# Softmax products moved from VectorE to GpSimd in every pair of a decoder layer, with GpSimd's own order changed around them

## The chip, the cores and the metric

One core of one Trainium2 chip. The metric is the device time of one execution in microseconds (us). In this document PE is TensorE's matrix multiply and PEld its weight load, DVE is VectorE, ACT is ScalarE, POOL is GpSimd, and SP is the engine that only issues DMAs.

## What is computed

One decoder layer on 16 sequences of 56 tokens with width 512, each with its own context of 1500 rows:

```
x = x + self_attention(layernorm(x))          # 32 heads of 16, 8 key/value heads, causal, softmax
x = x + cross_attention(layernorm(x), ctx)    # 16 heads, latent of 32, softmax over 1500 rows
x = x + ffn(layernorm(x))                     # one 512x512 product, a LoRA per sequence, bias
```

The part of the softmax that matters here is that of the self attention: row maximum, subtraction, exponential, row sum, reciprocal of the sum, and the product of the exponentials with it. The layer norm is (x - m) / sqrt(v + 1e-5) over 512 values.

## The kernel before, in words

The 16 sequences go in eight pairs, two sequences on 128 partitions (PAIRS is 8, B is 16). The whole is one software pipeline written out by hand: `run_bodies` calls `body(i)` for i from 0 to 8 on each engine, and a body has twelve steps g (0 to 11). In body i the cross attention of sequences 2i-1 (g 0 to 5) and 2i (g 6 to 11) runs, and between its pieces the list `STEPS` places the small operations of the self attention of pair n = i+1 and the end (output, ffn) of pair i-1. Every engine walks the same lists in the same order, so an engine that waits holds all that stands behind in its own order. Semaphores order the engines among each other.

The cross attention of a sequence is 24 units, numbered b * 24 + g * 4 + t, 12 for each half of the heads. For each unit PE makes scores (L741, into one of two PSUM banks `st_ps`), ACT takes the exponential (L993) into one of 8 slots of `p_ring`, PE multiplies by the context (L756) four units at a time, and POOL adds the slot onto `acc`, from which the denominators are made later (L1281). `add_up(b, half, since, until)` (L1264) is POOL's list of adds for a half: 11 adds, k from 1 to 11, where k = 1 takes two slots. ACT may write a slot again, 8 units later, only when its add is done (L992). PE also makes the pieces of the row maxima of the coming cross attention (L784, three banks `mx_ps`), 21 for each sequence, and DVE reduces each (L1210).

The self attention of pair n = i+1 in body i: PE makes the scores in steps SA and SB (g 3, L586), DVE adds the mask (L1123); then in two halves, k = 0 and 1, DVE takes the maximum (L1169) and subtracts it (L1171), ACT takes the exponential (SE0 and SE1 in g 4, L912), DVE sums (L1179), takes the reciprocal (L1184) and multiplies (L1186): `softmax_end`, called for SN0 at the end of g 4 and SN1 in g 5. PE transposes the product in g 6, steps P0 and P1 from the first half and P2 and P3 from the second (L594 to L604, recorded as L510). Two tables say which halves POOL does instead: `POOL_SHIFTS` for the subtraction (`shift`, L1299) and `POOL_SCALES` (L151) for the product (`scale`, L1306). In `POOL_SCALES` stand (0, 0) and (1, 0) alone, both done before the pipeline runs full. Where (n, k) is in it, DVE leaves the product out, POOL waits for DVE's reciprocal (`soft_n`, L1308), and PE waits for POOL (`scaled_po`, L595) in front of P0 or P2.

The three layer norms of each pair need 1/sqrt: POOL makes it in `power(which, n)` (L1284), three operations on one column each (L1289, L1292, L1296); the first waits for DVE's statistics (`mv`, L1072). ACT then normalises (L875, steps N0, N1, N2) and PE transposes the result. For the first norm (which = 0) that is step T1 in g 1 of the body. For the second (which = 1, the norm in front of the cross attention) the statistics come after step W1 in g 8 (L1132, L1068 to L1074), N1 stands in g 9 of ACT's list, and PE's T2 with the products CQ and H behind it in g 9 as well (L621 to L641).

POOL's order in a full body before the change is: `power(0, i+1)`, the 22 adds of sequence 2i-1, the 11 adds of the first half of 2i, `power(1, i+1)`, three adds, `power(2, i-1)`, the other eight adds.

Of the kernel before, what the change touches and what calls it, by code (L numbers as in the profile page):

```python
# [33 lines left out]
PAIRS = B // 2  # L34
# [113 lines left out]


POOL_SHIFTS = [(0, 0), (1, 0), (1, 1)]  # L150
POOL_SCALES = [(0, 0), (1, 0)]  # L151


LAST_STEPS = {6: ["XC"], 7: ["DN", "Y"], 8: ["DT"], 9: ["YT"], 10: ["T3"], 11: ["F1", "Fh", "F2"]}
# [9 lines left out]
def pool_adds(b, half):  # L164

    return ADDS * (b * 2 + half - sum(h < (b, half) for h in DVE_HALVES + [PE_HALF]))
# [14 lines left out]
def decoder_layer(nc, x, ctx_t, wq, wk, wv, wo, wq_d, w_qk, wkv_d, wv_u, gate_t, kern, bias,  # L181
                  lora_a, lora_b, lora_as, lora_bs, out):
    with ExitStack() as stack:
# [321 lines left out]
        def _(pe):  # L505
# [32 lines left out]
            def step(name, n, i=0, g=0):  # L538
# [50 lines left out]
                elif name in ("P0", "P1", "P2", "P3"):  # L589
                    r = int(name[1])  # L590
                    if r == 0:

                        pe.wait_ge(ct_sb, 2 * n + 1)
                    if r % 2 == 0 and (n, r // 2) in POOL_SCALES:  # L594
                        pe.wait_ge(scaled_po, POOL_SCALES.index((n, r // 2)) + 1)  # L595
                    elif r % 2 == 0:
# [465 lines left out]
        def _(ve):  # L1062
# [111 lines left out]
            def softmax_end(n, k):  # L1174
# [5 lines left out]
                ve.wait_ge(soft_n, 6 * n + 3 * k + 1)  # L1180
                if (n, k) in POOL_SCALES:
                    ve.reciprocal(inverse, total).then_inc(soft_n, 2)
# [79 lines left out]
        def _(po):  # L1262

            def add_up(b, half, since=1, until=ADDS):  # L1264

                if (b, half) in DVE_HALVES:
                    return
                if 0 <= b < B:
                    base = pool_adds(b, half)
                    dst = acc[:, b // 2 % 2, half * 8:(half + 1) * 8, b % 2 * SLOT:b % 2 * SLOT + S]  # L1270
                for k in range(since, until + 1):
                    if 0 <= b < B:
                        unit = (b * 2 + half) * 12 + k
                        po.wait_ge(exp_done, unit + 1)
                        if k == 1:

                            first = p_ring[:, (unit - 1) % PR, :].rearrange("p (h s) -> p h s", s=S)
                        else:
                            po.wait_ge(acc_done, base + k - 1)
                            first = dst  # L1280
                        po.tensor_tensor(dst, first, p_ring[:, unit % PR, :].rearrange("p (h s) -> p h s", s=S),  # L1281
                                         ALU.add).then_inc(acc_done, 1)

            def power(which, n):  # L1284

                if not 0 <= n < PAIRS:
                    return
                po.wait_ge(ln[which], (3 * n + 2, 4 * n + 3, 5 * n + 4)[which])
                po.tensor_tensor(rstd[:, which, 0:1], mv[:, which, 1:2], eps_col[:, :], ALU.add)\  # L1289
                    .then_inc(ln_eps[which], 1)  # L1290
                po.wait_ge(ln_eps[which], n + 1)
                po.tensor_tensor(rstd[:, which, 1:2], rstd[:, which, 0:1], minus_half[:, :], ALU.pow)\  # L1292
                    .then_inc(ln_pow[which], 1)
                po.wait_ge(ln_pow[which], n + 1)
                po.wait_ge(ln_neg[which], n + 1)
                po.tensor_tensor(rstd[:, which, 2:3], mv[:, which, 2:3], rstd[:, which, 1:2], ALU.mult)\  # L1296
                    .then_inc(ln_shift[which], 1)

            def shift(n, k):  # L1299

                po.wait_ge(soft, 4 * n + 2 * k + 2)
                rows = p1[:, k * 2 * G:(k + 1) * 2 * G, 0:S]
                po.tensor_tensor(rows, rows, sm[:, 0, k * 2 * G:(k + 1) * 2 * G].unsqueeze(2)
                                 .to_broadcast([128, 2 * G, S]), ALU.subtract).then_inc(shifted_po, 1)

            def scale(n, k):  # L1306

                po.wait_ge(soft_n, 6 * n + 3 * k + 3)  # L1308
                rows = p1[:, k * 2 * G:(k + 1) * 2 * G, 0:S]
                po.tensor_tensor(rows, rows, sm[:, 2, k * 2 * G:(k + 1) * 2 * G].unsqueeze(2)  # L1310
                                 .to_broadcast([128, 2 * G, S]), ALU.mult).then_inc(scaled_po, 1)
# [3 lines left out]
            def make(instruction):  # L1315

                made[0] += 1
                instruction.then_inc(pool_c, 1)
                po.wait_ge(pool_c, made[0])
# [31 lines left out]
            power(1, 0)  # L1351

            def body(i):
                power(0, i + 1)
                if i == 0:

                    po.wait_ge(eff_out, 32)
                    make(po.memset(acc[:, :, :, :], 1.0))
                    assert made[0] == ALL_MADE
                    for half in range(2):  # L1360
                        shift(1, half)
                    scale(1, 0)

                if i < PAIRS:
                    for half in range(2):
                        add_up(2 * i - 1, half)
                add_up(2 * i, 0)
                power(1, i + 1)
                add_up(2 * i, 1, until=3)
                power(2, i - 1)  # L1370
                add_up(2 * i, 1, since=4)

            run_bodies(body)


# [38 lines left out]
```

## Time and profile before

| what | value |
|---|---|
| median of 3 runs | 643.24 us |
| lowest, highest | 636.33, 643.40 us |
| the profiled execution, its own time | 636.64 us |
| span in its trace, first to last instruction | 634.8 us |
| mean granted TensorE clock | 0.984 |
| busy in the span: PE, DVE, ACT, POOL | 576.5, 404.4, 323.2, 426.6 us |

The times of rows in the trace count from the start of the span. The three runs lie at two levels, one at 636.33 us and two near 643.3 us; the profiled execution is near the lower one. A full body takes about 71.5 us (the power of the second norm comes at 236.26 us in body 2 and at 522.48 us in body 6). In timeline rows the columns are start, duration (both us), engine, line, operation, output and inputs, shapes, count; in brackets the idle time of the engine before and what ended it.

### The profile page before, as it was taken

To read this page: it belongs to the slowest core of one execution; us is meant where nothing else is said; L and a number is where in the kernel's file an instruction comes from. 1 tells how busy PE (TensorE), PEld (TensorE's weight loads), DVE (VectorE), ACT (ScalarE), POOL (GpSimd) and SP (SyncE) were. 2 spreads that over 40 slices of the span, in tenths; PEclk is the share of its full clock that TensorE was granted. 3 is DMA by queue.
4 is the path that set the end of the run, shared out by engine and by line. 5 is a ranking of instruction groups with operands and counts; after the bars stand their busy time and mean duration, and the time that the engine had idled before them with its cause. 6 is when DMAs were issued, how large, how long until landed. Compare 5 with 4: busy or idle time off the path is not lost.

```text
span 634.8 us, 11587 instructions
## 1 busy us (share of the span) xinstructions
PE 576.5 (91%) x4164; PEld 310.1 (49%) x4164; DVE 404.4 (64%) x696; ACT 323.2 (51%) x680; POOL 426.6 (67%) x414
## 2 busy tenths in 40 slices
PE   8887797999999899999999999999999899986886
PEld 7435343545446445545446444545446445433444
DVE  2536772688746955688746955688746965757532
ACT  1421445457544745557544745557544745564561
POOL 6202477589748888589748888588748878798000
PEclk9997898999999999999999999999999999999899
DMA  8959602651067201751059101751059101200000
GB/s 322 413 119 351 228 16 52 240 199 42 8 205 263 65 8 34 273 199 44 7 165 325 42 10 34 272 199 43 5 168 329 42 7 34 59 14 0 24 3 14
DMA packets 31579, 77.40 MB, mean 122 GB/s; under 512 B 11297, under 2 KB 24961, under 8 KB 29218
## 3 DMA queue, kind: packets, MB, share of 16 engines
q1 hardware_dynamic: 30854, 75.27, 35.0%
q10 hardware_dynamic: 668, 1.40, 0.6%
q8 instruction: 33, 0.54, 0.4%
q14 instruction: 24, 0.20, 0.1%
HBM read 58.92 MB, written 2.88 MB: 97 GB/s over the span
## 4 chain that ended last, share of the span: by engine, by line
PE 54%; DVE 23%; ACT 5%; SPq 5%; POOL 4%; issue 4%; DMA 4%; ACTq 1%; POOLq 0%; DVEq 0%
PE st_ps L741 9%; PE mx_ps L784 9%; PE pv_ps L756 8%; DVE mx_p L1210 7%; PE mi_ps L510 4%; PE mi_ps L522 4%; POOL acc L1281 4%; ACT p_ring L993 3%; DVE p L1123 2%; DMA x3n<-in_lora_b 2%; PE mi_ps L614 2%; DVE stats L1068 2%; SPq L422 2%; DVE p L1171 2%; PE mi_ps L618 2%
## 5 line engine op out<-in xcount | busy, mean ns | idle before, releaser
L1281 POOL TENSOR_TENSOR acc<-acc,p_ring 125x448 f32<-125x448 f32 x290 | 349.8, 1206 | 49.0 <-ACT p_ring L993 9.8
L1210 DVE TENSOR_REDUCE mx_p<-mx_ps 128x1 f32<-128x500 f32 x336 | 210.8, 671 | 109.2 <-PE mx_ps L784 108.1
L993 ACT ACTIVATE p_ring<-st_ps 125x448 f32<-125x448 f32 x372 | 184.3, 543 | 139.6 <-PE st_ps L741 132.9
L741 PE MATMUL st_ps<-q_st,c_st 98*125 98x448 f32 x372 | 144.7, 428 | 10.2 <-ACT p_ring L993 9.2
L784 PE MATMUL mx_ps<-c_st,q_st 96*128 96x500 f32 x336 | 139.6, 446 | 11.7 <-DVE p L1123 4.4
L741 PEld LDWEIGHTS st_ps<-q_st,c_st 98*125 98x125 f32 x372 | 64.6, 188 | 98.4 <-ACT p_ring L993 76.2
L756 PE MATMUL pv_ps<-p_ring,c_nat 125*32 125x448 f32 x768 | 93.5, 559 | 1.9 <-ACT ox L871 1.0
L784 PEld LDWEIGHTS mx_ps<-c_st,q_st 96*128 96x128 f32 x336 | 62.1, 192 | 44.3 <-DVE mx_p L1210 19.0
L1289 POOL TENSOR_TENSOR rstd<-mv,eps_col 128x1 f32<-128x1 f32 x24 | 5.0, 207 | 115.7 <-DVE mv L1072 115.2
L529 PE MATMUL mi_ps<-ctx_sb,wkv_sb 128*32 128x375 f32 x480 | 46.0, 504 | 3.8 <-DVE p L1123 3.8
L1159 DVE TENSOR_TENSOR x3n<-mi_ps,x 128x512 f32<-128x512 f32 x8 | 5.5, 691 | 53.9 <-PE mi_ps L725 53.9
L1281 POOL TENSOR_TENSOR acc<-p_ring 125x448 f32<-125x448 f32 x29 | 34.0, 1174 | 1.6 <-ACT p_ring L993 1.6
L871 ACT ACTIVATE qt<-mi_ps 128x512 f32<-128x512 f32 x16 | 9.6, 597 | 46.4 <-PE mi_ps L522 41.6
L522 PEld LDWEIGHTS mi_ps<-xnt,wq_sb 128*128 128x128 f32 x256 | 30.8, 192 | 0.8
L522 PE MATMUL mi_ps<-xnt,wq_sb 128*128 128x112 f32 (+1 forms) x256 | 30.8, 274 | 0.0
L756 PEld LDWEIGHTS pv_ps<-p_ring,c_nat 125*32 125x32 f32 x768 | 15.4, 108 | 30.0 <-issue 22.1
L1186 DVE TENSOR_TENSOR p<-p,sm 128x896 f32<-128x896 f32 x14 | 26.0, 1858 | 0.5
L529 PEld LDWEIGHTS mi_ps<-ctx_sb,wkv_sb 128*32 128x32 f32 x480 | 13.0, 112 | 25.0 <-issue 17.8
L1123 DVE TENSOR_TENSOR p<-mi_ps,cmask 128x448 f32<-128x448 f32 x32 | 18.4, 617 | 6.5 <-PE mi_ps L586 6.5
L871 ACT ACTIVATE ct_f<-mi_ps 128x375 f32<-128x375 f32 x15 | 7.2, 483 | 26.4 <-PE mi_ps L529 20.8
L871 ACT ACTIVATE p1t<-mi_ps 128x512 f32<-128x512 f32 x32 | 17.6, 604 | 4.1 <-PE mi_ps L510 4.1
L510 PE MATMUL mi_ps<-ident,p 128*128 128x128 f32 x128 | 18.0, 275 | 1.3 <-ACT p1t L871 0.3
(146 smaller groups left out, 678.7 us busy)
## 6 DMA issues: line engine op xcount, KB each, us to landing
ctx_sb<-in_ctx_t SPq DMA_DIRECT2D x16, 3000.0 KB, 11.2
c_st<-ct_hl SPq DMA_DIRECT2D x192, 46.9 KB, 2.3
q_st<-q_hl SPq DMA_DIRECT2D x90, 56.0 KB, 2.0
x_sb<-in_x SPq DMA_DIRECT2D x8, 256.0 KB, 2.8
out_y<-x3n SPq DMA_DIRECT2D x16, 112.0 KB
wq_sb<-in_wq SPq DMA_DIRECT2D x2, 512.0 KB, 6.0
kern_sb<-in_lora_a SPq DMA_DIRECT2D x1, 1024.0 KB, 14.5
wo_sb<-in_wo SPq DMA_DIRECT2D x1, 1024.0 KB, 17.4
```

What stands on the lines that cost most here:

```text
L510: last = pe.transpose(bank_[:, c * 128:(c + 1) * 128], src[:, c * 128:(c + 1) * 128], ident[:, :])
L522: last = mm(rows_of(o[:, r * 128:(r + 1) * 128], n), wq_sb[:, c, r * 128:(r + 1) * 128], rows_of(xnt[:, c, :], n), start=(c == 0), stop=(c ...
L529: last = mm(o[t * L:(t + 1) * L, 0:KT], wkv_sb[:, c, :], ctx_sb[:, slot, c, t * KT:(t + 1) * KT], start=(c == 0), stop=(c == CH - 1))
L741: mm(st_bank(unit)[0:KC, 0:HALF], c_st[:, b % 4, t * KT + k * KC:t * KT + (k + 1) * KC], q_st[:, b // 2 % 2, b % 2, half * HALF:(half + 1) ...
L756: last = mm(pv_ps[t * L:(t + 1) * L, 0:HALF], c_nat[:, b % 4, k, t * L:(t + 1) * L], p_ring[:, unit % PR, :], start=(k == 0), stop=(k == K ...
L784: mm(mx_ps[(b * PIECES + p) % MXB][:, 0:KP], q_st[0:96, b // 2 % 2, b % 2, j * 128:(j + 1) * 128], c_st[0:96, b % 4, k * KP:(k + 1) * KP], ...
L871: return act.activation(dst, src, ACT.Copy, scale=scale)
L993: act.activation(p_ring[:, unit % PR, :], st_bank(unit)[0:KC, 0:HALF], ACT.Exp, scale=float(L) ** -0.5).then_inc(exp_done, 1)
L1123: ve.tensor_tensor(rows[:, j:j + 2, half, :, 0:S], mi_ps[half][:, 0:G * S].rearrange("p (r g k) -> p r g k", r=2, g=G // 2), mask, ALU.add ...
L1186: ve.tensor_tensor(rows, rows, inverse.unsqueeze(2).to_broadcast([128, 2 * G, S]), ALU.mult)\
L1210: ve.tensor_reduce(mx_p[:, p:p + 1], mx_ps[unit % MXB][:, 0:KP], AX.X, ALU.max).then_inc(red_done, 1)
L1281: po.tensor_tensor(dst, first, p_ring[:, unit % PR, :].rearrange("p (h s) -> p h s", s=S), ALU.add).then_inc(acc_done, 1)
```

## The change

The table `POOL_SCALES` is longer, so that the 13 halves (1, 1), (2, 0), (2, 1) to (7, 1) have their products on POOL; DVE keeps that of (0, 1) alone. POOL's body is reordered: in bodies 1 to 7 the first add of sequence 2i-1 stands ahead of `power(0, i+1)`; in bodies 1 to 6 `scale(i+1, 0)` stands between the adds k = 5 and 6 of the second half of 2i-1, and `scale(i+1, 1)` between k = 7 and 8. In body 0 `scale(1, 1)` stands behind `scale(1, 0)`.

```diff
-POOL_SCALES = [(0, 0), (1, 0)]
+POOL_SCALES = [(0, 0)] + [(n, k) for n in range(1, PAIRS) for k in range(2)]
...
             def body(i):
-                power(0, i + 1)
                 if i == 0:
+                    power(0, 1)
 
                     po.wait_ge(eff_out, 32)
                     make(po.memset(acc[:, :, :, :], 1.0))
                     assert made[0] == ALL_MADE
                     for half in range(2):
                         shift(1, half)
-                    scale(1, 0)
-
-                if i < PAIRS:
                     for half in range(2):
-                        add_up(2 * i - 1, half)
+                        scale(1, half)
+
+                if 0 < i < PAIRS:
+                    add_up(2 * i - 1, 0, until=1)
+                    power(0, i + 1)
+                    add_up(2 * i - 1, 0, since=2)
+                    add_up(2 * i - 1, 1, until=5)
+                    if i + 1 < PAIRS:
+                        scale(i + 1, 0)
+                    add_up(2 * i - 1, 1, since=6, until=7)
+                    if i + 1 < PAIRS:
+                        scale(i + 1, 1)
+                    add_up(2 * i - 1, 1, since=8)
                 add_up(2 * i, 0)
                 power(1, i + 1)
                 add_up(2 * i, 1, until=3)
```

## Rows read from the trace of the kernel before

**Rows 1.** The page: busy time of each engine, and the chain that ended last.

```profile
PE 576.5 (91%) x4164; PEld 310.1 (49%) x4164; DVE 404.4 (64%) x696; ACT 323.2 (51%) x680; POOL 426.6 (67%) x414
...
PE 54%; DVE 23%; ACT 5%; SPq 5%; POOL 4%; issue 4%; DMA 4%; ACTq 1%; POOLq 0%; DVEq 0%
```

**Rows 2.** The waits of the whole span: who waited, total, times, longest.

```profile
POOL rstd L1289 <- DVE mv L1072: 115.2, 17, 35.5
...
PEld mx_ps L784 <- DVE mx_p L1210: 19.0, 42, 2.8
...
ACT p_ring L993 <- POOL acc L1281: 6.2, 7, 2.5
```

**Rows 3.** One line's instructions: duration min/median/max in ns, first and last start.

```profile
L1281 POOL TENSOR_TENSOR acc<-acc,p_ring x290: 1127/1141/1988, 79.4 to 583.8; 125x448 f32<-125x448 f32 x145
...
L1186 DVE TENSOR_TENSOR p<-p,sm x14: 1449/1868/2128, 23.0 to 503.9; 128x896 f32<-128x896 f32 x14
...
L1310 POOL TENSOR_TENSOR p<-p,sm x2: 1690/1690/1691, 22.5 to 75.7; 128x896 f32<-128x896 f32 x2
```

**Rows 4.** Timeline of POOL in body 2 (k = 5 first), 208.6 to 239 us.

```profile
208.57 1.15 POOL L1281 TENSOR_TENSOR acc<-acc,p_ring 125x448 f32<-125x448 f32 x1
...
209.86 3.93 POOL L1281 TENSOR_TENSOR acc<-acc,p_ring 125x448 f32<-125x448 f32 x2
...
214.28 6.33 POOL L1281 TENSOR_TENSOR acc<-acc,p_ring 125x448 f32<-125x448 f32 x4 [0.49 <-ACT p_ring L993]
...
220.57 1.16 POOL L1281 TENSOR_TENSOR acc<-p_ring 125x448 f32<-125x448 f32 x1
221.87 12.70 POOL L1281 TENSOR_TENSOR acc<-acc,p_ring 125x448 f32<-125x448 f32 x10
236.26 0.19 POOL L1289 TENSOR_TENSOR rstd<-mv,eps_col 128x1 f32<-128x1 f32 x1 [1.69 <-DVE mv L1072]
```

**Rows 5.** Timeline of DVE in body 2: the end of the softmax.

```profile
213.17 1.07 DVE L1179 TENSOR_REDUCE sm<-p 128x16 f32<-128x896 f32 x1
214.27 0.25 DVE L1184 RECIPROCAL sm<-sm 128x16 f32<-128x16 f32 x1
214.56 1.81 DVE L1186 TENSOR_TENSOR p<-p,sm 128x896 f32<-128x896 f32 x1
216.30 1.07 DVE L1179 TENSOR_REDUCE sm<-p 128x16 f32<-128x896 f32 x1
...
217.69 1.92 DVE L1186 TENSOR_TENSOR p<-p,sm 128x896 f32<-128x896 f32 x1
```

**Rows 6.** Timelines of PE and ACT in body 2: P2 and P3, a piece, T2, and N1.

```profile
219.93 1.06 PE L510 MATMUL mi_ps<-ident,p 128*128 128x128 f32 x8
...
237.59 0.47 PE L784 MATMUL mx_ps<-c_st,q_st 96*128 96x500 f32 x1
238.25 0.66 PE L510 MATMUL mi_ps<-ident,xn 128*128 128x128 f32 x4 [0.20 <-ACT xn L875]
...
237.38 0.82 ACT L875 ACTIVATE xn<-x_sb,rstd 128x512 f32<-128x512 f32 x1
```

**Rows 7.** Timelines of DVE and POOL: the same places in body 6.

```profile
500.48 0.25 DVE L1184 RECIPROCAL sm<-sm 128x16 f32<-128x16 f32 x1
...
498.02 1.98 POOL L1281 TENSOR_TENSOR acc<-acc,p_ring 125x448 f32<-125x448 f32 x1
...
522.48 0.19 POOL L1289 TENSOR_TENSOR rstd<-mv,eps_col 128x1 f32<-128x1 f32 x1 [1.69 <-DVE mv L1072]
```

**Rows 8.** One line's instructions: DVE's add onto x3, min/median/max in ns.

```profile
L1155 DVE TENSOR_TENSOR x<-x3n,x x8: 692/1670/1674, 166.9 to 620.8; 128x512 f32<-128x512 f32 x8
```

**Rows 9.** Stretches: length, busy of PE, PEld, DVE, ACT, POOL, then granted clock, DMA share, GB/s.

```profile
104.00:107.00 3.00, 0.93 (x3) 0.42 (x3) 0.00 (x0) 1.77 (x4) 2.46 (x3) 0.94 0.36 83
107.00:110.00 3.00, 3.00 (x12) 1.30 (x12) 1.36 (x2) 1.27 (x3) 2.70 (x3) 0.50 0.38 88
110.00:113.00 3.00, 3.00 (x15) 1.22 (x15) 0.68 (x1) 1.51 (x3) 0.71 (x1) 0.50 1.01 343
113.00:116.00 3.00, 3.00 (x31) 1.10 (x23) 1.40 (x3) 0.01 (x1) 0.00 (x0) 0.92 0.96 408
```

## The prediction

> **What bounds the kernel now.** I read the page first. PE is busy for 91% of the span, DVE for 64%, POOL for 67%, and the chain that ended last runs over PE for 54% and over DVE for 23% [rows 1]. So PE's own order sets the time, and another engine costs only where PE stands at a step and waits for it. Second I read the waits: POOL idles for 115.2 us in front of its powers, waiting for DVE's statistics, while ACT waits for POOL's adds for 6.2 us in all, and PE's weight loads wait for DVE's reductions for 19.0 us in 42 waits [rows 2]. POOL therefore has room in sum; the question is whether it has room where the products are put. Third I followed one full body (body 2, which makes pair 3 and has the steps of all bodies from 1 to 6) in the timelines of POOL, DVE, ACT and PE [rows 4 to 6].
>
> The time of a POOL add alone is 1.14 us (the median of 290), but some take up to 1.99 us, and DVE's product takes between 1.45 and 2.13 us [rows 3]. The timelines say why: the two engines take turns when DVE has two inputs in SBUF. DVE's product of 214.56 ends at 216.37, although it has 896 columns and the reduction over as many takes 1.07 us [rows 5]; it starts beside an add, the adds behind it get longer, and four of them take 6.33 us where four free ones take 4 x 1.14 + 3 x 0.14 = 4.99 (0.14 us is the gap between two adds: ten adds in 12.70 us [rows 4]). In the same way the two adds k = 6 and 7, beside the subtraction, take 3.93 us in place of 2.42 [rows 4].
>
> The Trainium skill (GPSIMD Engine Reference, 8. Key points) says that POOL shares its SBUF interfaces with DVE and that DVE instructions with two SBUF inputs contend; by this rule the change takes a conflict away, and the trace agrees (6.33 against 4.99 us). The same section says that elementwise work is about twice as fast on DVE, which speaks against the change.
>
> **The change part by part.** *DVE loses 13 products.* In body 2 these are 1.81 and 1.92 us [rows 5]. Nothing behind them is late: the next thing on DVE is a reduction of maxima that PE has only just made. On the path lies only P2, which PE starts at 219.93 [rows 6], about 0.3 us after the second product ends at 219.61 [rows 5]. Taken at nothing; at most 0.4 us a body. DVE's second sum (1.07 us) can follow the first reciprocal directly: it and its reciprocal (0.25 us) are done near 215.9.
>
> *POOL gets the products, and a wait in front of each.* A product costs 1.69 us on POOL [rows 3], both times measured with no DVE conflict. What is dear is the wait. POOL's add k = 5 ends at 209.72 [rows 4], and the next in its order is now `scale(3, 0)`, which needs the reciprocal that ends at 214.52 [rows 5]. POOL stands for 4.8 us. Before, it used 3.93 us of that for the adds k = 6 and 7 and idled for 0.49 [rows 4]. Nothing brings the reciprocal forward: what stands before it on DVE and ACT is unchanged. Body 6 has the same picture, k = 7 running from 498.02 while the reciprocal comes at 500.48 [rows 7].
>
> POOL's new row of work from the reciprocal on, with 0.1 us to start and no gap where an instruction does not wait for the one before: product 214.62 to 216.31; adds k = 6 and 7 (2.42) to 218.69; product to 220.34; adds 8 to 11 (4.99) to 225.29; the eleven adds of the first half of sequence 4, which took 220.57 to 234.57 [rows 4], so 14.00, to 239.25. Before they ended at 234.57: POOL is 4.7 us late. In parts: the row starts 0.3 us later (214.62 against 214.28), the two products are 3.3 us, the two adds now behind the wait 2.4 us, and 1.3 us of conflict in the four adds is gone (6.33 less 4.99).
>
> *Who waits for that.* The next in POOL's order is `power(1, 3)`, which stood idle for 1.69 us and started at 236.26 [rows 4]. It now starts at about 239.2, 3.0 us late. N1 on ACT started 1.12 us after it (237.38), and T2 on PE started when N1 was done, at 238.25 [rows 6]. PE was free at 238.06 and nothing behind T2 can pass it. So T2 and all after it move by 3.0 us. There may be 0.5 us more: DVE's add onto x3 (0.69 us when it has the port alone, 1.67 at the median [rows 8]) now falls just at POOL's last add and the power, and one of them gives way. P2 waits for the second product until 220.4 in place of 219.93: 0.5 us, but this is inside the 3.0, since PE then waits less at T2. The exponentials of g 7 come up to 1.6 us late for want of ring slots (the one that needs add k = 11, done at 225.29, ran at 223.84), but PE's steps there have other work and catch up before g 9. Nothing after T2 gives it back, for PE works without a gap from H to the end of the ffn.
>
> *How many times.* Bodies 1 to 6, with T2 of pairs 2 to 7: six. Body 6 shows the same 1.69 us of room as body 2 [rows 7]. Bounds for one body: 2.4 us, where gaps are smaller and PE catches up a little after the stall; 3.6 us with the whole turn-taking at the power. I take 3.1: six make 18.6 us, between 14.4 and 21.6.
>
> *The first add ahead of power(0, i+1).* It uses 1.28 us of an idle stretch; the adds behind come 1.28 us earlier, but ACT waits for adds for only 6.2 us in the whole span [rows 2], and by k = 4 of the second half POOL waits for ACT again. Nothing; at most 1 us in all. *Body 0*: one more product (1.69 us) ahead of the adds, less 0.8 us of conflict, under the room before power(1, 1); DVE's backlog of reductions starts a little earlier. Between -0.5 and +0.5 us, taken at nothing.
>
> *The clock.* PE now stands at T2 from about 238.5 to 241.3. Where PE was little busy at 104 to 107 us (0.93 of 3 us), the granted clock then was 0.50 for 6 us and 0.92 for 3 more [rows 9]: against 2.4 GHz, 3 x 0.06 + 3 x 0.5 + 3 x 0.5 + 3 x 0.08 = 3.4 us of PE's work lost. A stall of 2.8 us in each body can do the same. Bounds: nothing, or six times 3.4 = 20.4 us. I expect it in some of the six, at half the price since PE is not all that counts behind T2: two times 1.7, so 3.4 us.
>
> The Trainium skill (TensorE: Matmul & The Clock Gate, Part 1) has a gate that halves the clock after idleness; rows 9 agree, at 0.50. By that rule each stall at T2 is a candidate.
>
> **The sum.** 18.6 + 3.4 = 22 us, on the profiled execution's 636.64 (span 634.8): 658.6 us, or 3.5% more. The three runs lie at two levels, 636.33 and 643.3, and the median 643.24 is 6.6 us above the profiled execution. With two runs of three at the upper level the same sum gives 665. I name 663, nearer the upper one.
>
> **The rivals.**
> *A, the wait is hidden (no change).* If POOL did not stand before the product, the debt would be 2 x 1.65 - 1.5 (k = 6 and 7) - 1.3 = 0.5 us, less than the 1.69 us of room, and T2 would stay. That needs the reciprocal some 3 us earlier, near 211.5. For: 67% busy POOL. Against: rows 4 and 5, which put the reciprocal 4.8 us behind k = 5. Also here: PE catches up most of the stall, 1.5 us a body left. Time 643 - 2 to 643 + 10.
> *B, faster.* DVE is what PE waits for: with 3.7 us a body off it, the 19.0 us of waits for reductions [rows 2] go, and 0.4 us x 6 at P2: at most 21 us, 622. It decides where PE waits for DVE for over 12.9 us in the g 6 to g 8 behind the products. Against: DVE itself waits for PE's pieces within 2 us of 219.5, and its backlog there is one piece.
> *C, the clock falls at every T2.* 18.6 + 6 x 1.7 to 6 x 3.4 = 29 to 39 us: 672 to 682. For: the stall is as long as those after which the clock fell. Against: busy work on both sides of it.
> *D, the change does nothing it says.* The table is read by DVE, POOL and PE alike; I give it no chance of its own.
>
> **How the numbers follow.** The forecast 0.60 (its own range 652 to 672), C 0.20, A 0.15, B 0.05. The range 645 to 677 leaves out B, the lower part of A and the upper part of C. A measurement of this kernel tells about 2% from no change, 12.9 us, so up to 656.1. The forecast lies under that in some 0.05 of its 0.60 and A is mostly within: faster 0.05, within 2% 0.18, slower 0.77.
>
> **What would show it.** In the profile after: POOL idle for about 4.8 us in front of L1310 in six bodies, on DVE's reciprocal; no idle time in front of the power of the second norm, where 1.69 us stood; N1 and T2 about 3 us late against the body's own start, with PE waiting 2.5 to 3.2 us for xn; a body of some 75 us in place of 71.5; adds k = 6 to 11 all near 1.14 us; DVE busy 24 us less, POOL about 5 us more (13 x 1.69 = 22, less six times 1.5 + 1.3). P2 waits for POOL for 0.5 us. It is wrong if T2's wait stays under 1 us, or if the body's length grows while PE waits elsewhere, or if the clock falls in most bodies.

## The result and the profile after

The changed kernel takes 670.42 us at the median of four runs (665.37 to 674.54), the kernel before 641.44 beside it (636.33 to 643.40). The ratio is 1.049, with a 95% interval of 1.045 to 1.054: slower, by about 30 us. The profiled execution took 667.74 us, 31.1 more than that of before.

The page of the changed kernel, busy times and the chain that ended last, answers to [rows 1]:

```profile
PE 591.8 (89%) x4164; PEld 320.9 (48%) x4164; DVE 378.4 (57%) x683; ACT 324.6 (49%) x680; POOL 429.6 (65%) x427
...
PE 45%; POOL 23%; DVE 10%; issue 9%; ACT 5%; DMA 4%; SPq 3%; ACTq 0%; POOLq 0%; DVEq 0%
```

DVE lost 26.0 us and POOL gained only 3.0, as the products went over and the turn-taking stopped. But POOL, 4% of the chain before, is now 23% of it, at a lower busy share than before. PE's busy time grew by 15.3 us with the same number of instructions: a sign of the clock. (The profiled execution of the kernel before, with a granted clock of 0.984, is near the fast end of its runs, so differences against it come out a little larger than the 29 us between the medians.)

The waits of the changed kernel (who waited, total, times, longest), for [rows 2]:

```profile
POOL rstd L1289 <- DVE mv L1072: 89.7, 11, 36.7
...
POOL p L1310 <- DVE sm L1182: 31.8, 7, 5.0
...
PE mi_ps L510 <- ACT xn L875: 18.1, 7, 3.1
...
ACT p_ring L993 <- POOL acc L1281: 14.1, 15, 4.5
PEld mx_ps L784 <- DVE mx_p L1210: 14.1, 29, 2.8
...
PEld mi_ps L510 <- POOL p L1310: 4.1, 5, 1.0
```

The new wait of POOL for DVE's reciprocal is there, 4.96 us in each of bodies 1 to 6. PE waits 18.1 us at the transposes for xn, 16.6 of them at T2 of these six bodies; before, the wait at T2 was 0.2 us a body [rows 6].

Timeline of POOL in body 2 of the changed kernel, for [rows 4]:

```profile
213.15 1.13 POOL L1281 TENSOR_TENSOR acc<-acc,p_ring 125x448 f32<-125x448 f32 x1
219.25 1.69 POOL L1310 TENSOR_TENSOR p<-p,sm 128x896 f32<-128x896 f32 x1 [4.96 <-DVE sm L1182]
220.90 2.41 POOL L1281 TENSOR_TENSOR acc<-acc,p_ring 125x448 f32<-125x448 f32 x2
223.27 1.69 POOL L1310 TENSOR_TENSOR p<-p,sm 128x896 f32<-128x896 f32 x1
224.92 5.01 POOL L1281 TENSOR_TENSOR acc<-acc,p_ring 125x448 f32<-125x448 f32 x4
229.89 1.15 POOL L1281 TENSOR_TENSOR acc<-p_ring 125x448 f32<-125x448 f32 x1
231.18 12.67 POOL L1281 TENSOR_TENSOR acc<-acc,p_ring 125x448 f32<-125x448 f32 x10
243.80 0.19 POOL L1289 TENSOR_TENSOR rstd<-mv,eps_col 128x1 f32<-128x1 f32 x1
244.07 0.55 POOL L1292 TENSOR_TENSOR rstd<-rstd,minus_half 128x1 f32<-128x1 f32 x1
244.70 0.68 POOL L1296 TENSOR_TENSOR rstd<-mv,rstd 128x1 f32<-128x1 f32 x1
```

Read from the wait downward: 4.96 us idle, then no gap at all until the power, in front of which 1.69 us of idle time stood. The adds k = 6 and 7 take 2.41 us where they took 3.93, and 8 to 11 take 5.01 where they took 6.33. DVE and PE in the same body:

```profile
218.92 0.25 DVE L1182 RECIPROCAL sm<-sm 128x16 f32<-128x16 f32 x1
...
220.22 0.25 DVE L1182 RECIPROCAL sm<-sm 128x16 f32<-128x16 f32 x1
225.29 1.35 DVE L1210 TENSOR_REDUCE mx_p<-mx_ps 128x1 f32<-128x500 f32 x2 [4.82 <-PE mx_ps L784]
...
244.64 0.69 DVE L1155 TENSOR_TENSOR x<-x3n,x 128x512 f32<-128x512 f32 x1
...
246.28 0.66 PE L510 MATMUL mi_ps<-ident,xn 128*128 128x128 f32 x4 [2.18 <-ACT xn L875]
```

The time that DVE was given it spends waiting for PE: 4.82 us here, where the clock had fallen (see below), and 3.28 to 3.29 us in the four bodies where it had not. T2 comes 27.11 us after the first reciprocal's end, at 219.17; before it was 23.73 (214.52 to 238.25, [rows 5, 6]). It is so in all six bodies (27.08 to 27.12 us). In four of them PE idles 3.07 us in front of T2. In the other two, bodies 2 and 6, it idles 2.18, since a slow clock in g 4 to g 6 had already made PE late.

Then the clock. Stretches of the changed kernel around T2 of body 1, columns as in [rows 9]:

```profile
163.00:166.00 3.00, 2.84 (x22) 1.42 (x19) 2.36 (x7) 1.52 (x3) 2.57 (x4) 1.00 0.00 0
166.00:169.00 3.00, 0.40 (x3) 0.10 (x1) 2.65 (x7) 0.39 (x1) 2.84 (x5) 1.00 0.01 3
169.00:172.00 3.00, 2.26 (x14) 1.49 (x14) 1.09 (x2) 1.89 (x5) 2.71 (x3) 0.66 0.00 0
172.00:175.00 3.00, 3.00 (x35) 2.20 (x36) 0.76 (x2) 0.80 (x3) 1.09 (x4) 0.50 0.00 0
175.00:178.00 3.00, 3.00 (x14) 1.17 (x14) 1.80 (x3) 1.92 (x4) 2.28 (x2) 0.70 0.16 38
178.00:181.00 3.00, 3.00 (x20) 1.45 (x19) 1.66 (x4) 2.52 (x6) 2.31 (x3) 1.00 0.33 77
```

PE is busy for 0.40 of 3 us, and the clock then is half (1.2 GHz) for some 7 us. It fell at T2 in six bodies of six: for about 7 us in the four with the stall of 3.07 us, for about half as long in the two with 2.18. In those two (at 221 and 528 us) it had also fallen in the steps g 4 to g 6 before. The mean granted clock went from 0.984 to 0.948.

A body now takes 76.75 us (five bodies, first reciprocal to first reciprocal, 142.39 to 526.13), before 71.57 (142.87 to 500.74): 5.17 more. Six times that is 31.0 us, the whole difference between the two profiled executions.

### The profile page after: what moved, and what is told of

Its sections match the earlier page's. It is cut to its first block, busy times and chain, and to the rows that moved or that the text cites. A ratio compares the mean times of both kernels' runs of the same rounds, so it can differ in the third digit from the quotient of the medians.

```text
span 665.9 us, 11600 instructions
## 1 busy us (share of the span) xinstructions
PE 591.8 (89%) x4164; PEld 320.9 (48%) x4164; DVE 378.4 (57%) x683; ACT 324.6 (49%) x680; POOL 429.6 (65%) x427
## 4 chain that ended last, share of the span: by engine, by line
PE 45%; POOL 23%; DVE 10%; issue 9%; ACT 5%; DMA 4%; SPq 3%; ACTq 0%; POOLq 0%; DVEq 0%
POOL acc L1281 20%; PE st_ps L741 8%; PE mx_ps L784 7%; PE pv_ps L756 7%; DVE mx_p L1210 4%; PE mi_ps L522 4%; PE mi_ps L510 3%; ACT p_ring L993 3%; DMA x3n<-in_lora_b 2%; PE mi_ps L639 2%; PE mi_ps L719 2%; DVE p L1123 2%; PE mi_ps L586 2%; PE mi_ps L723 2%; SPq L422 1%
## 5 line engine op out<-in xcount | busy, mean ns | idle before, releaser
L1281 POOL TENSOR_TENSOR acc<-acc,p_ring 125x448 f32<-125x448 f32 x290 | 330.3, 1139 | 65.7 <-ACT p_ring L993 29.4
L1210 DVE TENSOR_REDUCE mx_p<-mx_ps 128x1 f32<-128x500 f32 x336 | 213.5, 672 | 154.2 <-PE mx_ps L784 152.9
L741 PE MATMUL st_ps<-q_st,c_st 98*125 98x448 f32 x372 | 149.3, 441 | 11.9 <-ACT p_ring L993 10.8
L784 PE MATMUL mx_ps<-c_st,q_st 96*128 96x500 f32 x336 | 142.8, 458 | 10.4 <-DVE p L1123 4.4
L756 PE MATMUL pv_ps<-p_ring,c_nat 125*32 125x448 f32 x768 | 97.1, 579 | 1.9 <-ACT ox L871 1.0
L784 PEld LDWEIGHTS mx_ps<-c_st,q_st 96*128 96x128 f32 x336 | 64.6, 200 | 40.1 <-DVE mx_p L1210 14.1
L1310 POOL TENSOR_TENSOR p<-p,sm 128x896 f32<-128x896 f32 x15 | 25.3, 1688 | 31.8 <-DVE sm L1182 31.8
L529 PE MATMUL mi_ps<-ctx_sb,wkv_sb 128*32 128x375 f32 x480 | 43.8, 483 | 2.0 <-DVE p L1123 2.0
L510 PE MATMUL mi_ps<-ident,xn 128*128 128x128 f32 x64 | 11.0, 299 | 18.1 <-ACT xn L875 18.1
L875 ACT ACTIVATE xn<-x_sb,rstd 128x512 f32<-128x512 f32 x14 | 11.4, 815 | 19.1 <-POOL rstd L1296 19.0
```

The source lines that it names most:

```text
L510: last = pe.transpose(bank_[:, c * 128:(c + 1) * 128], src[:, c * 128:(c + 1) * 128], ident[:, :])
L529: last = mm(o[t * L:(t + 1) * L, 0:KT], wkv_sb[:, c, :], ctx_sb[:, slot, c, t * KT:(t + 1) * KT], start=(c == 0), stop=(c == CH - 1))
L741: mm(st_bank(unit)[0:KC, 0:HALF], c_st[:, b % 4, t * KT + k * KC:t * KT + (k + 1) * KC], q_st[:, b // 2 % 2, b % 2, half * HALF:(half + 1) ...
L756: last = mm(pv_ps[t * L:(t + 1) * L, 0:HALF], c_nat[:, b % 4, k, t * L:(t + 1) * L], p_ring[:, unit % PR, :], start=(k == 0), stop=(k == K ...
L784: mm(mx_ps[(b * PIECES + p) % MXB][:, 0:KP], q_st[0:96, b // 2 % 2, b % 2, j * 128:(j + 1) * 128], c_st[0:96, b % 4, k * KP:(k + 1) * KP], ...
L1210: ve.tensor_reduce(mx_p[:, p:p + 1], mx_ps[unit % MXB][:, 0:KP], AX.X, ALU.max).then_inc(red_done, 1)
```

## The experiments

Letters for theories in this section are its own and not those of the prediction. My theory W: POOL's wait in front of the first product makes its adds late, the power of the second norm stands behind these, PE stalls at T2, and the clock falls behind the stall. The rivals: the moved first add (O), the products' own time on POOL (P), the wait alone (Q), late adds and ring slots (R), a threshold in place of a gradual loss (T), a clock that falls for another reason than the stall or costs nothing beside it (C, K), a fill that holds nothing up, so that the stall itself costs more (F), and time saved on DVE that would show once POOL holds nobody up (D).

| run | median us | before beside it | ratio, 95% interval |
|---|---|---|---|
| e1_products_old_order | 668.93 | 638.75 | 1.046, 1.039 to 1.054 |
| e2_first_add_only | 639.73 | 638.75 | 1.000, 0.996 to 1.004 |
| e3_products_two_adds_later | 641.77 | 638.75 | 1.004, 1.000 to 1.008 |
| e4_fill_at_t2 | 663.45 | 638.75 | 1.038, 1.032 to 1.045 |
| e5_shorter_fill_at_t2 | 660.83 | 638.94 | 1.032, 1.026 to 1.038 |
| e6_wait_without_products | 658.51 | 638.94 | 1.028, 1.024 to 1.033 |
| e7_products_one_add_later | 652.55 | 638.94 | 1.021, 1.015 to 1.027 |
| e8_powers_ahead_of_adds | 642.23 | 638.94 | 1.005, 1.002 to 1.009 |
| e9_later_products_powers_ahead | 640.53 | 640.02 | 1.000, 0.997 to 1.003 |
| e10_wait_only_with_fill | 644.13 | 640.02 | 1.005, 1.002 to 1.008 |

**The order around the first norm's power, undone and alone.**

```diff
-                    add_up(2 * i - 1, 0, until=1)
                     power(0, i + 1)
-                    add_up(2 * i - 1, 0, since=2)
+                    add_up(2 * i - 1, 0)
```

> The changed kernel with power(0, i+1) back in front of the first add; the 13 products stay on POOL. Theory W (POOL's wait in front of the first product, and the clock that falls behind the stall at T2, make the whole loss): the moved add only fills idle time, so this run is within 2 us of the changed kernel, about 670 us, with T2 waiting 2.2 to 3.1 us in six bodies. Rival O (the new order around the first norm's power is part of the loss or pays some of it back): 3 us or more away from the changed kernel.

> The kernel before with the first add alone moved ahead of power(0, i+1); DVE keeps its products. Theory W: the time of the kernel before, within 0.3% (641 us, between 639 and 643). Rival O: over 0.5% away from it, 3 us or more.

668.93 us without it, within 2 us of the changed kernel, and a ratio of 1.000 with it alone. The moved add makes no difference beyond 0.4% (e2), O falls, and the loss comes with the products and where they stand.

**The products two adds later, and one add later.** The diff is that of e3; in e7 the first product stands behind k = 6 and the second behind k = 8.

```diff
-                    add_up(2 * i - 1, 1, until=5)
+                    add_up(2 * i - 1, 1, until=7)
...
-                    add_up(2 * i - 1, 1, since=6, until=7)
+                    add_up(2 * i - 1, 1, since=8, until=8)
...
-                    add_up(2 * i - 1, 1, since=8)
+                    add_up(2 * i - 1, 1, since=9)
```

> The changed kernel with the products placed behind adds k = 7 and k = 8 of the second half, so that POOL reaches the first when the reciprocal is nearly there (a wait of about 0.7 us, where 4.8 stood). Theory W: POOL's debt at the second norm's power shrinks from 4.7 us by about 3.9 (two adds at 1.28 and 1.14, and what they lose to the subtraction), so less than 1.5 us remains at T2, 0 to 1.2 us of stall in each body, and the clock falls in few bodies or none: 641 to 650 us. Rival P (the products' own 1.69 us on POOL, twice a body, are the loss, wherever they stand): the debt stays over 3.3 us less 1.7 of room, T2 waits at least 1.6 us, and the time is 655 us or more.

> The changed kernel with the first product behind k = 6 in place of k = 5 and the second behind k = 8: halfway to the run with the products two adds later (641.8 us). Theory W: one add (1.28 us) less behind the wait than in the changed kernel, one more than in that run, so T2 is 1.3 to 1.6 us late in each body, a stall of about 1.5 us: 8 to 10 us, and a clock that falls in some bodies, up to 6 us more: 650 to 658 us. Rival T (a threshold: either POOL hides everything or the whole loss is there): within 3 us of 642 or within 4 us of 670.

With the same 13 products on POOL, two adds further down its list, 641.77 us: all but 3 us of the loss is gone. POOL's timeline of that run, body 2:

```profile
213.41 1.69 POOL L1310 TENSOR_TENSOR p<-p,sm 128x896 f32<-128x896 f32 x1 [0.89 <-DVE sm L1182]
215.05 1.14 POOL L1281 TENSOR_TENSOR acc<-acc,p_ring 125x448 f32<-125x448 f32 x1
216.15 1.69 POOL L1310 TENSOR_TENSOR p<-p,sm 128x896 f32<-128x896 f32 x1
217.80 3.70 POOL L1281 TENSOR_TENSOR acc<-acc,p_ring 125x448 f32<-125x448 f32 x3
...
235.38 0.19 POOL L1289 TENSOR_TENSOR rstd<-mv,eps_col 128x1 f32<-128x1 f32 x1
```

The wait is 0.89 us where 4.96 stood, and the power comes 22.06 us after the reciprocal (213.32), 0.3 us later than before. T2 waits 0.58 us and the clock does not fall in bodies 1 to 6. So P falls: 3.4 us of products a body fit into POOL's room. One add more behind the wait (k = 7, in e7) gives 652.55, between the two and within the 650 to 658 expected, against a threshold (T). PE idles 1.31 to 1.33 us at T2 in all six bodies, and the clock fell behind four of them. Body 3 of e7, T2 and then the stretches behind it:

```profile
314.92 0.66 PE L510 MATMUL mi_ps<-ident,xn 128*128 128x128 f32 x4 [1.33 <-ACT xn L875]
```

```profile
316.00:318.00 2.00, 1.73 (x17) 1.02 (x21) 1.93 (x7) 0.49 (x2) 1.86 (x3) 0.64 0.00 0
318.00:320.00 2.00, 2.00 (x34) 1.63 (x27) 0.60 (x2) 0.51 (x1) 0.80 (x3) 0.51 0.00 0
```

**PE kept busy at T2.** `fill(20, o)` makes 20 matmuls of the identity that nobody reads, in T2's own bank; e5 has 13 in place of 20.

```diff
                 elif name == "T2":
 
+                    if n >= 2:
+                        pe.wait_ge(ln[1], 4 * n + 1)
+                        fill(20, o)
                     pe.wait_ge(ln[1], 4 * n + 4)
```

> The changed kernel with 20 matmuls of the identity onto itself put in front of T2 in bodies 1 to 6, as soon as T2's bank is free, so that PE is busy in the stall (about 2.2 us of work). They leave the output as it is. Theory W: the stall itself stays (POOL is as late), but the granted clock stays at 1.00 behind T2; the loss goes from about 30 us to the 3.0 us a body of the stall: 656 to 662 us. Rival C (the clock falls for another reason than the stall, or costs nothing beside the stall): no gain, 668 us or more.

> The run with the fill again, with 13 matmuls in place of 20. In that run 20 took 4.66 us, not 2.2, and T2 began at 248.73 while xn was ready at 247.44: the fill itself held T2 for 1.2 us a body. 13 should take 3.0 us and end before xn. Theory W: the clock stays at 1.00 in bodies 1 to 6, T2 starts when xn is ready, and the 663 us fall by six times 1.2: 656 us, between 653 and 659, which leaves some 14 us as the clock's part of the changed kernel's loss and 16 as the stall's. Rival F (the fill did not hold T2, the stall's own price is 3.7 us a body): no change, 661 us or more.

With 20 matmuls 663.45 us, 1.5 us above my range, and a clock of 1.00 in all of bodies 1 to 6. The fill was too long: each matmul took 0.23 us, and T2 began 1.3 us after xn was ready. With `fill(13, o)` it ends in time in four bodies (PE's timeline of body 2):

```profile
243.28 3.06 PE L536 MATMUL mi_ps<-ident 128*128 128x128 f32 x26
246.52 0.66 PE L510 MATMUL mi_ps<-ident,xn 128*128 128x128 f32 x4 [0.17 <-ACT xn L878]
```

660.83 us, over my range (653 to 659) and by the number on the edge of F's 661; with four runs of each, e4 and e5 also overlap (657.12 to 662.20 against 659.96 to 666.02). The traces decide. In two bodies (at 295 and 446 us) the clock fell all the same, in g 4 to g 6. PE came late to the fill there, the fill held T2 for about 2.4 us after xn was ready, and these bodies took 75.8 and 75.9 us. The three bodies measured without any fall took 74.24 us at the mean, where the bodies of e4 take 75.4. So the long fill did hold T2, and F falls. Behind T2 the clock held in all six.

These 74.24 us are 2.67 more than before. By this estimate the stall's own price is six times 2.67, 16 us, and the rest of the 31.1, 15 us, is the clock's. A part of the 15, at most some 2 us, lies in the end of the kernel and not in the six bodies: from the last T2 on it took 112.65 us, before 110.33, and the clock was slow there for longer too.

**The wait alone, and the wait alone with the fill.** POOL's table goes back, so that DVE multiplies, but POOL waits where `scale` stood:

```diff
-POOL_SCALES = [(0, 0)] + [(n, k) for n in range(1, PAIRS) for k in range(2)]
+POOL_SCALES = [(0, 0), (1, 0)]
...
-                        scale(i + 1, 0)
+                        po.wait_ge(soft_n, 6 * (i + 1) + 2)
...
-                        scale(i + 1, 1)
+                        po.wait_ge(soft_n, 6 * (i + 1) + 5)
```

> The changed kernel's order of POOL with DVE keeping the products of all pairs from 2 on and of (1, 1): POOL only waits for the two reciprocals, behind k = 5 and k = 7, and multiplies nothing. Theory W: POOL is 2.7 us late at the end of the adds, less the 1.7 us of room: T2 about 1.0 us later in each body, hardly a stall that drops the clock: 645 to 650 us; so wait and products each fill the room and only together make the stall. Rival P (the products' time is the loss, the wait alone costs nothing): 641 us. Rival Q (the wait alone is the loss): over 655 us.

658.51 us, above the 645 to 650 that I expected: by the number this is rival Q's run. The wait alone, without one product on POOL, brings 20 of the 30 us. My sentence that wait and products only together make the stall was wrong. Its timelines, POOL and then PE in body 2, and the stretches behind:

```profile
217.69 3.32 POOL L1281 TENSOR_TENSOR acc<-acc,p_ring 125x448 f32<-125x448 f32 x2 [4.89 <-DVE sm L1184]
...
240.73 0.19 POOL L1289 TENSOR_TENSOR rstd<-mv,eps_col 128x1 f32<-128x1 f32 x1
```

```profile
240.68 0.47 PE L784 MATMUL mx_ps<-c_st,q_st 96*128 96x500 f32 x1
242.71 0.74 PE L510 MATMUL mi_ps<-ident,xn 128*128 128x128 f32 x4 [1.57 <-ACT xn L875]
```

```profile
240.00:242.00 2.00, 0.98 (x6) 0.58 (x5) 1.22 (x4) 0.63 (x2) 1.84 (x5) 1.00 0.00 0
242.00:244.00 2.00, 1.16 (x5) 0.67 (x5) 1.90 (x6) 2.00 (x4) 1.86 (x2) 0.79 0.00 0
244.00:246.00 2.00, 1.86 (x15) 1.16 (x19) 0.83 (x3) 0.36 (x2) 1.86 (x3) 0.50 0.00 0
```

POOL's power comes 23.12 us after the reciprocal (217.61) in place of 21.74, 1.4 us late where I had worked out 1.0. The stall was nearly as expected, but behind 1.57 us of idle PE the clock fell as behind 3.07, in the five bodies that had such a stall. (In body 4, where a fall in g 4 to g 6 had made PE late, PE idled 0.19 us at T2 and the clock held there.) I had taken it to hold. To see that this was the difference, e10 adds six idle matmuls to e6:

> The run in which POOL only waits for the reciprocals and multiplies nothing (658.5 us), with 6 matmuls of the identity in front of T2, 1.4 us, where PE stood for 1.55. They leave the output as it is. Theory W, as amended: POOL's power comes 1.4 us late there, 6 x 1.4 = 8.4 us, and the rest of the 19.6 us is the clock, which fell behind T2 in five of six bodies; with the fill the clock stays and 647 to 650 us remain. Rival K (the clock falls in these bodies for other reasons than the stall at T2): 655 us or more.

```diff
+                    if n >= 2:
+                        pe.wait_ge(ln[1], 4 * n + 1)
+                        fill(6, o)
```

644.13 us, below the 647 to 650 expected. Six idle matmuls a body take 14 us off. T2 is as late as in e6 (PE's timeline, body 3, where the reciprocal ended at 289.26), and the stretch behind it has its clock:

```profile
312.63 1.50 PE L536 MATMUL mi_ps<-ident 128*128 128x128 f32 x12
314.34 0.66 PE L510 MATMUL mi_ps<-ident,xn 128*128 128x128 f32 x4 [0.21 <-ACT xn L878]
```

```profile
314.00:316.00 2.00, 1.33 (x13) 0.89 (x13) 1.90 (x7) 1.63 (x4) 1.86 (x2) 1.00 0.00 0
316.00:318.00 2.00, 2.00 (x42) 1.41 (x38) 1.06 (x2) 0.57 (x2) 1.78 (x4) 1.00 0.00 0
```

So of e6's 20 us the stall itself is about 4, less than the 8 I expected, and the clock 14 and more. K falls. T2 is 1.35 us later than before in these bodies, but the next body starts only about 0.5 us later: PE makes up the rest behind T2, as in e5.

**The powers ahead of the adds.** The waits and products stay; only what stands behind them changes:

```diff
-                add_up(2 * i, 0)
-                power(1, i + 1)
-                add_up(2 * i, 1, until=3)
-                power(2, i - 1)
-                add_up(2 * i, 1, since=4)
+                if 0 < i < PAIRS - 1:
+                    add_up(2 * i, 0, until=8)
+                    power(1, i + 1)
+                    add_up(2 * i, 0, since=9)
+                    power(2, i - 1)
+                    add_up(2 * i, 1)
...
```

(In the other bodies the order stays as it was.)

> The changed kernel, products and waits as they are, with the second norm's power put ahead of the last three adds of the first half of 2i and the third norm's power right behind these. POOL is as late with its adds as before (4.7 us), but the powers no longer stand behind them. Theory W: T2 does not wait for xn beyond 0.3 us, the clock stays, and only P2's half microsecond is left: 641 to 646 us. Rival R (the loss comes from late adds: ring slots that ACT waits for, and PE behind it): the adds are as late as in the changed kernel, so most of the loss stays, 655 us or more.

642.23 us. POOL's timeline, body 2:

```profile
218.17 1.69 POOL L1310 TENSOR_TENSOR p<-p,sm 128x896 f32<-128x896 f32 x1 [4.96 <-DVE sm L1182]
...
230.10 8.81 POOL L1281 TENSOR_TENSOR acc<-acc,p_ring 125x448 f32<-125x448 f32 x7
240.32 0.19 POOL L1289 TENSOR_TENSOR rstd<-mv,eps_col 128x1 f32<-128x1 f32 x1 [1.41 <-DVE mv L1072]
```

The wait of 4.96 us is still there and the adds are as late, but the power waits for its statistics again, and all but 3.3 us of the loss is gone (the interval, 1.002 to 1.009, leaves a little; P2's half microsecond a body was expected to stay). This is the cleanest of the runs: R falls. It also says how far Q holds: the wait as such costs almost nothing, and what it cost came through the second norm's power that stood behind it.

**Both repairs.**

> Both repairs together: the products behind k = 7 and k = 8, and the two powers placed as in the run with the powers ahead of adds. Theory W: T2 waits for nothing but the statistics, and P2 no longer waits for DVE's second product (0.3 to 0.4 us a body before): 636 to 640 us, the kernel before or up to 0.4% under it. Rival D (DVE's freed 3.7 us a body are worth something once POOL holds nobody up): 634 us or less.

The edits of e3 and e8 together: 640.53 against 640.02, a ratio of 1.000 (0.997 to 1.003), over 12 runs. That is half a microsecond above the 636 to 640 expected. With POOL holding nobody up, what DVE was relieved of is worth nothing that can be measured. D falls, and none of these versions beats the kernel before.

## Why the prediction was right, and where it was off

It said slower, with 22 us (3.5%) of loss, 663 us and a range of 645 to 677; measured were 670.42 us and 4.9%. The direction, the wait and the path to T2 were as written. The clock was not: "if the clock falls in most bodies" stands among the prediction's own signs of being wrong, and it fell in all six. The traces show its rival C, which it gave 0.20: 31 us of loss in the profiled execution, where C says 29 to 39. That 670.42 lies in the range, just under C's 672 to 682, owes something to luck: the stall came out 2.6 us smaller than its term, and 4.4 us had been added without ground (see below). By the steps:

- *DVE's products cost nothing to lose and bring nothing*: held. DVE waits 3.3 us and more for PE where it multiplied, and e9 shows the relief to be worth nothing that can be measured. So rival B, that PE waits for DVE, was not there to be won: PE's waits for reductions fell from 19.0 to 14.1 us while the kernel got slower.
- *POOL's wait, 4.8 us*: 4.96. *POOL's new row of work, 24.7 us from the reciprocal to the last add* (214.52 to 239.25): 24.67 (219.17 to 243.84). *Power 3.0 us late*: 24.63 less 21.74, 2.9 us. *Perhaps 0.5 us more from turn-taking at the power*: it came; the power's last operation took 0.68 us in place of 0.19, beside DVE's add onto x3 of 244.64. T2 was 3.4 us late, 2.9 and 0.5.
- *Nothing after T2 gives it back*: this was wrong by some 0.6 us a body. A body without a fall of the clock is 2.67 us longer, not 3.4, and the timelines of e5 have the third-norm and next-pair steps 2.8 us late from the transpose of the maxima (MT) on: some 0.6 us is made up between H and MT. The sum of this term, 18.6 us, measured about 16, and its range of 2.4 to 3.6 a body held. In e10, 0.9 of 1.35 us is made up.
- *The clock, 3.4 us*: the term that failed. I expected it in some of the six bodies, at half the price of one fall. It fell behind T2 in all six and twice elsewhere, and cost about 15 us. The mechanism stood in the working, with rows 9 and rival C; how often it strikes and so its size were wrong, by a factor of four. C's own term, 10.2 to 20.4 us, holds the 15. From (1 - 0.948) x 665.9 = 34.6 us against (1 - 0.984) x 634.8 = 10.2, some 24 us of PE's full clock were lost, of which 15 showed in the time. I argued that busy work on both sides of a stall protects it; e7 and e6 show the clock falling behind 1.31 and 1.57 us of idle PE amid the same work.
- *663 in place of 658.6*: the step of 4.4 us for a kernel before that runs "at two levels" has no ground. The 23 runs of it beside e9 lie all over 636.75 to 643.28 us, with no gap above 1.3 us between neighbours. This step brought the number nearer to the measured one by luck.
- *A product's 1.69 us, "measured with no DVE conflict"*: a misreading without effect on the sum. In both cases DVE's own product starts beside it (at 23.00 and 76.84 us, POOL's at 22.50 and 75.66); POOL's keeps its 1.69 us and DVE's gets longer, 2.13 us for the first.
- *P2 waits half a microsecond for POOL*: the five waits of 4.1 us are one of 0.34 in body 0 and four of 0.94 to 0.96 us, where P2 waited 0.39 for DVE before: 0.56 more, hidden in T2's stall as said. In bodies 2 and 6 PE came late and did not wait. *The first add ahead of the power: nothing*: shown by e1 and e2, within 0.4%.
- Rival A's condition, a reciprocal near the place where POOL stands, is what e3 makes: the time is then that of the kernel before, within 0.4%.

Left open: why the clock falls in g 4 to g 6 in some bodies and some runs (twice in the profile after, twice in e5, once each in e6, e8 and e10, never in bodies 1 to 6 of the kernel before, e3 and e9). It was not tried.

## What to carry to other kernels

When an instruction with a wait goes into an in-order engine, look at what stands behind it and which of that is on somebody's path: here 4.96 us of waiting was free once one small operation had moved ahead (e8), or once the wait stood where its data were ready (e3). Price the engine's debt against the idle time in front of the next operation that matters (1.69 us), not against its busy share of 67%. A stall of PE has two prices, its length and the clock behind it, and the second can be the larger. A few matmuls that compute nothing tell the two apart in one run (e6 against e10, 14 us).

## What was not expected of the hardware

- The granted clock fell to half behind an idle stretch of PE of only 1.31 to 1.33 us (four bodies of six in e7) and 1.55 to 1.58 us (five of five in e6), and held where 1.5 us of matmuls stood in its place (e10).
- A matmul of the 128x128 identity in f32 took 0.23 us there (3.06 us for 13, recorded as 26), twice what I had expected for e4.
- An operation of POOL on a single column, 0.19 us, took 0.68 us beside DVE's addition with two inputs in SBUF, which took its 0.69 us; POOL's adds fell from 3.93 to 2.41 us a pair when DVE's subtraction no longer ran beside them.
